# Vision tower, second attention: GpSimd scales the probabilities head by head, four multiplies a pair in place of two

## The reference

```python
def _mhsa(q, k, v, scale):
    s = jnp.einsum('ghid,ghjd->ghij', q, k) * scale
    a = jax.nn.softmax(s, axis=-1)
    return jnp.einsum('ghij,ghjd->ghid', a, v)
...
qkv = (layernorm(h) @ W_qkv)       # split into q, k, v per head
out = _mhsa(q, k, v, dh ** -0.5)   # 197 x 197 scores for each head
h = h + out @ W_0
```

## Time and profile before

| | before |
|---|---|
| median of three runs | 2645.27 us |
| profiled execution, its own time | 2642.03 us |
| its span in the trace | 2640.2 us |
| second attention | about 829 to 2397 us of the span |
| TensorE, VectorE, ScalarE, GpSimd busy | 93%, 83%, 79%, 41% |
| granted TensorE clock in the second attention | 1.00 (2.4 GHz) |
| GpSimd's multiply (L1349) | 768 instructions, 840 ns each, 625.0 us |

### The profile page before, as it was taken

The page is one execution under the profiler, slowest core; times in us unless marked ns, Lnnn a source line. Parts: engine busy times, 40 slices in busy tenths (PEclk is TensorE's granted clock), DMA queues, the critical chain, the costliest instruction groups (busy, mean ns, idle before and its releaser), DMA issues. The chain is left out here.

```text
span 2640.2 us, 83428 instructions
## 1 busy us (share of the span) xinstructions
PE 2458.9 (93%) x27552; PEld 2112.2 (80%) x27552; DVE 2198.4 (83%) x5761; ACT 2094.3 (79%) x6199; POOL 1084.7 (41%) x1501
## 2 busy tenths in 40 slices
PE   5889977999997999999999999999999999996876
PEld 4778865877885888888888888888888888885665
DVE  6776768988776888888888888888888888887997
ACT  3677766777765888888888888888888888887998
POOL 5777732333331343443443333333334434341333
PEclk9999978999998999999999999999999999999999
DMA  5334400010002333333333333333333333330111
GB/s 172 110 104 117 119 19 25 0 40 5 0 0 56 81 73 69 83 69 69 83 69 72 80 71 73 76 76 73 71 80 71 69 83 69 69 83 10 45 43 51
DMA packets 181839, 173.22 MB, mean 66 GB/s; under 512 B 19206, under 2 KB 180432, under 8 KB 181520
## 3 DMA queue, kind: packets, MB, share of 16 engines
q1 hardware_dynamic: 181776, 172.44, 27.6%
HBM read 46.49 MB, written 9.68 MB: 21 GB/s over the span
## 5 line engine op out<-in xcount | busy, mean ns | idle before, releaser
L1349 POOL TENSOR_TENSOR b_pr<-b_pr,b_rinv 128x394 f32<-128x394 f32 (+1 forms) x768 | 625.0, 840 | 990.5 <-DVE b_rinv L1307 990.5
L1244 ACT ACTIVATE b_pr<-b_banks,b_nmx 128x197 f32<-128x197 f32 (+1 forms) x1536 | 626.8, 423 | 37.2 <-DVE b_nmx L1301 28.9
L1301 DVE TENSOR_REDUCE b_nmx<-b_banks 128x2 f32<-128x394 f32 (+1 forms) x768 | 395.7, 557 | 64.1 <-PE b_banks L1170 60.3
L1154 PE MATMUL b_banks<-b_xt,wqkv 128*128 128x197 f16 x3840 | 384.8, 250 | 4.8 <-DVE b_xt L1272 2.2
L1154 PEld LDWEIGHTS b_banks<-b_xt,wqkv 128*128 128x128 f16 x3840 | 318.4, 98 | 36.3 <-issue 18.9
L1180 PE MATMUL b_bank_t<-ident,b_pr 128*128 128x128 f32 (+3 forms) x3072 | 333.3, 250 | 5.4 <-DVE b_pt L1272 4.6
L1170 PE MATMUL b_banks<-b_kst,b_qst 128*128 128x197 f16 (+1 forms) x3072 | 326.5, 248 | 3.3 <-DMA b_kst<-b_qk 1.8
L1244 ACT ACTIVATION_READ_ACCUMULATOR b_pr<-b_banks,b_nmx 128x1 f32 (+1 forms) x1536 | 312.4, 203 | 0.0
L1180 PEld LDWEIGHTS b_bank_t<-ident,b_pr 128*128 128x128 f32 (+3 forms) x3072 | 287.0, 141 | 25.1 <-issue 10.8
L1170 PEld LDWEIGHTS b_banks<-b_kst,b_qst 128*128 128x128 f16 (+1 forms) x3072 | 264.8, 105 | 22.8 <-issue 11.0
L442 PE MATMUL tokens<-tok_w,parts 128*128 128x192 f16 (+1 forms) x2304 | 212.5, 254 | 57.2 <-POOL parts L314 57.2
(11 more groups left out here) (235 smaller groups left out, 4843.7 us busy)
## 6 DMA issues: line engine op xcount, KB each, us to landing
b_qst<-b_qk SPq DMA_DIRECT2D x512, 147.8 KB, 2.6
b_kst<-b_qk SPq DMA_DIRECT2D x512, 73.9 KB, 2.3
patches<-in_x SPq DMA_DIRECT2D x64, 588.0 KB, 4.3
out<-z_res SPq DMA_DIRECT2D x32, 192.0 KB
out<-z_res SPq DMA_DIRECT2D x32, 103.5 KB
m_raw_weights<-in_wqkv SPq DMA_DIRECT2D x2, 1152.0 KB, 6.6
m_raw_weights<-in_w SPq DMA_DIRECT2D x2, 576.0 KB, 5.1
h<-in_fc SPq DMA_DIRECT2D x1, 768.0 KB, 5.7
```

The source lines that it names most:

```text
L1154: last = t.matmul(out[:, g * SEQ:(g + 1) * SEQ], w[:, (2 * n + g) * P:(2 * n + g + 1) * P], x, start=(j == 0), stop=(j == 4))
L1244: last = nc.scalar.activation(pr[n % 3][0:ROWS[c], c, e, :], banks[0:ROWS[c], c, e * SEQ:(e + 1) * SEQ], ACT.Exp, bias=nmx[n % 2][0:ROWS[c ...
L1301: v.reduce_max(nmx[n % 2][0:ROWS[c], c, :], banks[0:ROWS[c], c, 0:2 * SEQ].rearrange("p (e t) -> p e t", e=2), AX.X, negate=True).then_inc ...
L1349: last = nc.gpsimd.tensor_tensor(p, p, inv, ALU.mult)
```

## The change

Each chunk's multiply is cut into two, one for each head. Before, one instruction covered 2 x 197 columns, with the two reciprocals repeated 197 times each by the access pattern; after, an instruction covers 197 columns of one head with the one reciprocal of that head. The buffers, the waits and the place of the increment (after the last multiply of the pair) are the same.

```diff
                     for c in range(2):
                         p = pr[n % 3][0:ROWS[c], c]
-                        inv = rinv[n % 2][0:ROWS[c], c, :].unsqueeze(2).to_broadcast([ROWS[c], 2, SEQ])
-                        last = nc.gpsimd.tensor_tensor(p, p, inv, ALU.mult)
+                        for e in range(2):
+                            inv = rinv[n % 2][0:ROWS[c], c, e:e + 1].to_broadcast([ROWS[c], SEQ])
+                            last = nc.gpsimd.tensor_tensor(p[:, e], p[:, e], inv, ALU.mult)
                     last.then_inc(prob_made, 1)
```

## The result

| | before | after |
|---|---|---|
| median of 8 runs each | 2645.61 us (2644.63 to 2648.74) | 2654.41 us (2652.19 to 2655.71) |
| profiled execution, its own time | 2642.03 us | 2654.95 us |
| its span | 2640.2 us | 2653.2 us |
| start of the first and of the last of the transposes in the second attention | 832.3 to 2395.3 us | 832.3 to 2405.0 us |
| a turn of its loop (two images) | 49.10 us | 49.355 us |

The change makes the kernel slower by a ratio of 1.0032, 95% interval 1.0021 to 1.0042: 8.8 us, with 5.6 to 11.1 us as the interval. Forecast were 15.5 us, 2660.8 us in all, with a range of 2648 to 2669. The sign, the place and the price of a multiply came out as forecast, but only a bit over half of the time, 8.8 of 15.5 us.

The account below looks back on a forecast made before the run. TensorE was taken to bound the second attention, at 24.55 us an image. 64 x 0.29 - 3.4 = 15.2 us at pair 5, plus 0.3 for the first image's pair 3, gave 15.5 us: 2660.8 us, range 2648 to 2669.

Parts of the forecast that it names:

- pair 5 alone has no room: Second attention: of six pairs an image, only pair 5's product ends just before TensorE's transposes, 0.13 and 0.08 us ahead.
- 0.29 us more a pair: GpSimd's multiplies: four of 197 columns take 1.94 us a pair in place of 1.64, two fixed parts more.
- The low bound: GpSimd's price from the 192 and 384 column adds: 0.05 us fixed an operation, 0.10 us a pair.
- rival A: GpSimd's fixed part is small in long operations: 0.10 us a pair, 3.1 us in all, 2648.4; chance 0.07.
- The upper bound: GpSimd's durations added up, overlap lost: a pair takes 2.06 us, 0.42 more, 24 us in all.
- Free at pair 5: 0.03 and 0.08 us: Room between GpSimd's product and TensorE's transposes after a 0.05 us signal: 0.08 in a turn's first image, 0.03 in the other.
- there whatever GpSimd does: TensorE's gap of 0.05 us between scores and pair 5's transposes, in one image a turn, claimed independent of GpSimd.
- I find no stall of TensorE elsewhere in the turn that could give it back.: Rest of the loop turn: no TensorE wait was expected to absorb pair 5's delay, so all of it was counted.
- rival D: TensorE's queue makes up pair 5's stall at a later point: 2645 to 2650 us; chance 0.04.
- The forecast's own case: GpSimd's four multiplies cost 0.2 to 0.42 us more a pair, 9.6 to 24 us in all; chance 0.80.
- Everything off the path costs nothing: Other pairs' later products stay within their room (pair 3: 0.29 of 0.70 us); GpSimd's 111 us more fit its idle stretches.
- Contention: GpSimd slowed beside VectorE work, as adds in the MLP (4.33 us for 2.22); here no overlap was expected: nothing.

Follow-up runs that it names:

- runs with pair 5 alone: Kernel before with only pair 5 of each image multiplied in four operations, the other pairs in two: 2654.48 us against 2643.95, ratio 1.0039.
- run with one multiply: Kernel before with one multiply a pair over all four row blocks (128 x 788 columns) in place of two: 2643.23 us against 2643.95, ratio 0.9999.
- run without pair 5: Kernel before with pairs 0 to 4 multiplied in four operations and pair 5 in two: 2645.91 us against 2643.95, ratio 1.0009.
- the three with the other order: Kernel before with VectorE's pair 5 reciprocal earlier and TensorE's fourth values piece later; two, four, one multiplies a pair: 2652.12, 2652.05, 2655.71 us against 2643.88.
- two kernels with the same instructions: Kernel before, and the same with the second attention's loop begun one image later: 2643.18 us (one execution) against 2643.88.
- the run with the shorter VectorE row: Kernel before, two multiplies, VectorE's low half of the values' fourth piece cut from 384 columns to 8: 2637.67 us against 2643.50, ratio 0.9977.
- both reorderings: Against kernel before: one multiply, pair 2's scores ahead of pair 0's transposes, 1.0050; two multiplies, VectorE's pair 5 reciprocal earlier, TensorE's fourth values piece later, 1.0036.

## Why the prediction was right, and where not

- **TensorE's pace bounds the stage, and pair 5 alone has no room.** Right: the runs with pair 5 alone and without it.
- **0.29 us more a pair, two fixed parts of 0.147.** Right: 0.28 (1.924 against 1.640 from the instructions' starts and ends). The multiplies start 0.471 apart (forecast 0.474) and last 0.511. The line through 8 and 394 columns also holds at 98 and 99 (0.308 apart, forecast 0.311) and at 788 (0.14 less than two of 394). The low bound, from the 192 and 384 column adds, was off, and so was rival A. The upper bound, durations added up, was off too: as the Trainium skill has it (Perfetto Trace Analysis, section GPSIMD Engine Instruction), the spacing of starts is what counts. On the price of an instruction the Trainium skill (GPSIMD Engine Reference, section Instruction dispatch) gives tens of cycles for one indirect call, one of several stages. The whole fixed part that the runs show is 0.14 us, so the estimate of 50 ns from that call was too low for a whole instruction.
- **Free at pair 5: 0.03 and 0.08 us.** The first is right: a stall of 0.25 in the other image of the turn is 0.284 less 0.03. The second is wrong: in the image that opens a turn nothing was free. GpSimd's signal takes 0.134 us there before and after alike, and the gap called "there whatever GpSimd does" was GpSimd's, as the run with one multiply shows. This missed 0.08 x 30 = 2.4 us, towards too small a cost.
- **The step that failed: "I find no stall of TensorE elsewhere in the turn that could give it back."** There was one before pair 0, for VectorE's low half of pair 5: 0.28 us a turn with its echo in the transposes, 0.28 x 30 = 8.4 us. This is rival D in part, to which I gave 0.04 with "no idle time of TensorE in rows 2" against it. The row can't tell that. The loop's cost is 0.255 x 30 = 7.7 us in place of 0.47 x 30 = 14.1; the stage as a whole grew by 2405.0 - 2395.3 = 9.7 us, the last 2 outside the loop, nearly all of it ahead of it, where two kernels with the same instructions differ by 1.5 us as well. The parts add up: 14.1, plus the 2.4 above, less 8.4 of cover and 0.4 for the price (0.284 in place of 0.29), are 7.7.
- **The range.** That 8.8 us lies in it is luck in part. The forecast's own case, 0.2 to 0.42 us a pair, was 9.6 to 24 us, and 8.8 is below it although the price of a pair was right. The range reached lower for rival A, a cheap multiply, which isn't what happened; nothing in it allowed for the cover.
- **Everything off the path costs nothing.** Right: the run without pair 5, and the three with the other order.
- **Contention: "beside VectorE's normalisation in the MLP" four adds took 4.33 us.** The outcome (nothing) was right, the reading of the earlier trace rows wasn't. The normalisation had ended at 558.75 + 0.34 = 559.09, before the adds began at 559.28; VectorE was then at L896. The adds at 406.50 met no work of VectorE and took 0.585 us each, nearly all that began while L896 was running 0.91 or more. So the price of contention came from a neighbour that this stage doesn't have, and no trace here shows what the normalisation would cost.

```profile
558.75 0.34 DVE L117 TENSOR_SCALAR m_xn<-h,mean,rstd 69x128 f32<-69x128 f32 x1
559.00 1.52 DVE L896 TENSOR_TENSOR m_hid<-m_act,m_hid 128x394 f16<-128x394 f32 x3
```

The profiled span grew by 13.0 us, of which the stage holds 9.7. The other 3.3 lie in stages that the change doesn't touch, and within the scatter of executions.

No version here beats the kernel before and computes the same. The run with the shorter VectorE row shows the size of what lies behind pair 0 (5.8 us by the medians, 0.263 us a turn), but it leaves out part of the computation; both reorderings that were to get at it made another arrival late. Whether some order gets it stays open.

## What to carry to other kernels

Before pricing a delay on the critical engine, look at the step from start to start of each group of its matmuls against the same group's unhindered step; busy shares and lists of waits hide waits of 0.1 us, and in this kernel such a wait for another engine was cover for a delay ahead of it. Where two chains end at one engine within 0.1 or 0.2 us of each other, as here, lengthening one costs its excess less this cover, once, and then in full; shortening the one that TensorE doesn't wait for last gained nothing (one multiply), and shortening the other gained the cover (0.263 us a turn). Splitting a GpSimd operation cost a fixed 0.14 us for each further piece, which matters only where its product is waited for at once.

## What the runs showed of the hardware

- A GpSimd multiply with a repeated factor costs 0.14 us and 1.6 to 1.7 ns a column, from 98 to 788 columns, on 69 and on 128 partitions alike (511 ns at 197 columns on both).
- TensorE starts 0.055 us behind the end of the GpSimd operation that it waits for, and 0.134 us behind it right after the start of a loop's turn, in every kernel in which it waited there.
- In the changed kernel GpSimd's multiplies beside VectorE's work of this stage took 505 to 517 ns each, all 1536: no trace of contention. In the MLP a GpSimd add of 192 columns took 0.585 us with VectorE idle, and in nearly all cases 0.91 us or more when it began while VectorE's L896 was running.
